# Diagonal blocks of the row maxima: the causal mask moves from a matmul to a GpSimd addition, with a copy on ScalarE between, and the maxima are taken for two heads at once

## The reference

```python
h = _layernorm(x, axis=-1) * (1 + ca) + sa
# attention, for each of 16 heads:
scores = jnp.einsum('bhqd,bhkd->bhqk', q, k) * scale
scores = jnp.where(causal, scores, jnp.finfo(scores.dtype).min)
attn = jax.nn.softmax(scores, axis=-1)
out = jnp.einsum('bhqk,bhkd->bhqd', attn, v)
...
x = x + ga * attention(h)
h = _layernorm(x, axis=-1) * (1 + cb) + sb
x = x + gb * soft_mixture_of_experts(h)
```

## Time and profile before

| | |
|---|---|
| Three runs | 3223.44, 3226.12, 3234.1 us; median 3226.12 |
| The profiled execution | 3226.97 us |
| Its span, first to last instruction | 3225.1 us |
| Granted TensorE clock, mean | 0.986 |
| Busy share: PE, PEld, DVE, ACT, POOL | 94%, 48%, 70%, 54%, 11% |

### The profile page before, as it was taken

One profiled execution on the slowest core, in us unless ns is written; L12 is line 12 of the kernel. 1 busy time (PEld: TensorE's weight loads), 2 busy tenths in 40 slices (PEclk: granted clock), 3 DMA queues, 4 the chain that ended last, 5 costly groups with the idle time before them and its releaser, 6 DMA issues.

```text
span 3225.1 us, 45179 instructions
## 1 busy us (share of the span) xinstructions
PE 3028.2 (94%) x17474; PEld 1535.5 (48%) x17651; DVE 2249.3 (70%) x4388; ACT 1754.8 (54%) x3189; POOL 340.8 (11%) x196
## 2 busy tenths in 40 slices
PE   6699999989999999998999999999999999999899
PEld 4233334447653333454774333345477333334468
DVE  5888887572778878756388888866448888885722
ACT  3356666564236666645515666664541666665550
POOL 4100000320400000112040000011222000002200
PEclk9899999999999999999999999999999999999999
DMA  5222201015412220002542202000453221100052
GB/s 153 79 41 41 41 1 40 15 57 205 150 35 34 41 41 27 21 7 92 196 138 54 41 1 41 28 21 7 145 178 116 41 41 26 17 27 27 33 180 75
DMA packets 124260, 206.12 MB, mean 64 GB/s; under 512 B 10223, under 2 KB 107189, under 8 KB 120425
## 3 DMA queue, kind: packets, MB, share of 16 engines
q1 hardware_dynamic: 110460, 153.07, 14.5%
q10 hardware_dynamic: 13584, 50.15, 8.4%
HBM read 160.21 MB, written 42.19 MB: 63 GB/s over the span
## 4 chain that ended last, share of the span: by engine, by line
PE 76%; DVE 15%; ACT 5%; issue 2%; ACTq 1%; DMA 1%; POOL 0%; SPq 0%; DVEq 0%
PE ps L737 14%; DVE pm L1347 12%; PE ps L717 9%; PE ps L642 9%; PE ps L904 7%; PE ps L843 7%; PE ps L655 7%; PE ps L935 4%; PE ps L602 3%; PE ps L924 3%; ACT R L1047 2%; PE ps L783 2%; PE ps L676 2%; PE ps L634 2%; PE ps L856 2%
## 5 line engine op out<-in xcount | busy, mean ns | idle before, releaser
L1347 DVE TENSOR_REDUCE pm<-ps 128x1 f32<-128x512 f32 (+4 forms) x2560 | 1380.5, 603 | 292.1 <-PE ps L642 193.5
L1047 ACT ACTIVATE R<-ps 128x512 f32<-128x512 f32 (+1 forms) x2240 | 1177.3, 592 | 652.0 <-PE ps L717 425.0
L717 PE MATMUL ps<-R 99*128 99x512 bf16 (+3 forms) x2560 | 829.8, 350 | 17.6 <-ACT R L1047 7.8
L642 PE MATMUL ps<-R 96*128 96x512 bf16 x1536 | 580.9, 386 | 39.4 <-DVE pm L1347 34.6
L737 PE MATMUL ps<-R 128*17 128x512 f32 (+3 forms) x5120 | 531.6, 533 | 4.9
L642 PEld LDWEIGHTS ps<-R 96*128 96x128 bf16 x1536 | 147.7, 97 | 437.3 <-DVE pm L1347 363.0
L717 PEld LDWEIGHTS ps<-R 99*128 99x128 bf16 x2560 | 241.9, 98 | 155.1 <-ACT R L1047 67.1
L655 PE MATMUL ps<-R 128*128 128x257 f32 x1024 | 247.2, 382 | 7.2 <-ACT R L991 3.6
L737 PEld LDWEIGHTS ps<-R 128*17 128x17 f32 x5120 | 118.2, 97 | 281.9 <-issue 168.4
L904 PE MATMUL ps<-R 128*128 128x512 f32 x512 | 230.0, 611 | 18.0 <-ACT R L1119 18.0
L843 PE MATMUL ps<-snT,R 128*128 128x512 f32 x512 | 230.1, 593 | 0.0
(11 more groups left out here) (159 smaller groups left out, 3142.8 us busy)
## 6 DMA issues: line engine op xcount, KB each, us to landing
R<-in_L_ffn_w_dram SPq DMA_DIRECT2D x64, 1024.0 KB, 6.1
R<-q_parts ACTq DMA_DIRECT2D x12, 768.0 KB
R<-k_parts ACTq DMA_DIRECT2D x12, 768.0 KB
q_parts<-R SPq DMA_DIRECT2D x16, 512.0 KB, 3.6
k_parts<-R SPq DMA_DIRECT2D x16, 512.0 KB, 3.5
R<-in_L_attn_x_dram SPq DMA_DIRECT2D x4, 2048.0 KB, 8.7
x_park<-R SPq DMA_DIRECT2D x16, 512.0 KB, 2.6
R<-x_park SPq DMA_DIRECT2D x16, 512.0 KB, 5.5
```

Source lines behind the costliest of these rows:

```text
L642: last = mm(ps[:, bank, :], qt(4 * c + r), kt(4 * kc, 4), start=True, stop=True)
L717: last = mm(bank[:, i * w:(i + 1) * w], kst[g % 2][0:BROWS, h0 + i, j * P:(j + 1) * P], qst[g % 2][0:BROWS, h0 + i, (c + 1) * CH - w:(c + ...
L1047: A(Eb[s % ESLOTS][:, h0:h0 + n, 0:w], ps[:, u % NST, 0:n * w].rearrange("p (n w) -> p n w", n=n), ACT.Exp, scale=SCALE).then_inc(s_ex, 1)
L1347: mx = lambda o, i: V.tensor_reduce(o, i, AX.X, ALU.max)
```

## The change

- PE writes a diag unit without the mask: four matmuls, each starting its part of the bank anew.
- ACT copies the bank to SBUF (`copied_diagonal`), in one of two buffers `mdiag`, each for a pair of heads. The bank is free for PE after this copy.
- POOL adds `maskb` in place (`masked_diagonal`).
- DVE reduces a pair at once, 128 x 1024 to eight maxima: heads 0 and 1 after the "even" unit of head 1, heads 2 and 3 after the chunk's last unit and before `negmax`.
- In `MAXES` the diag unit of head `h + 1` stands before the "odd" unit of head `h`.
- PE waits, three places back, for ACT's copy (`s_dgc`) or DVE's reduction (`s_mxf`), whichever kind of unit that was.
- `mdiag` lies on memory that a rotary set uses, so the first copy of a batch waits for the transfers that park that set.
- In the turn of a batch ACT's last rotary conversions (`parts(b + 1, 7)`) and its stores stand between the copies.

```diff
 def max_units_of_chunk(k):
     c = k % NC
+    yield k, 0, "diag", 0, 0
     for h in range(HG):
-        yield k, h, "diag", 0, 0
+        if h + 1 < HG:
+            yield k, h + 1, "diag", 0, 0
         yield k, h, "odd", 0, 0
...
-                pe.wait_ge(s_mxf, b * MU + (m + 1))
+                if m >= NMX:
+                    if m - NMX in DIAGONALS:
+                        pe.wait_ge(s_dgc, b * ND + diagonals_to(m - NMX))
+                    else:
+                        pe.wait_ge(s_mxf, b * DU + others_to(m - NMX))
...
                 elif kind == "diag":
-                    mm(ps[:, bank, :], identb[:, :], maskb[:, :, :].rearrange("p r t -> p (r t)"),
-                       start=True, stop=True)
                     for i in range(4):
-                        last = mm(ps[:, bank, i * P:(i + 1) * P], qt(4 * c + i), kt(4 * c + i, 1),
-                                  start=False, stop=True, skip_group_check=True)
+                        last = mm(ps[:, bank, i * P:(i + 1) * P], qt(4 * c + i), kt(4 * c + i, 1), start=True, stop=True)
...
+            def copied_diagonal(b, m):
+                if MAXES[m][2] != "diag":
+                    return
+                i = DIAGONALS.index(m)
+                if i == 0:
+                    act.wait_ge(s_pk[2], set_parked(b, max(j for j in range(QU) if set_of(b, j) == 2)))
+                if i >= 4:
+                    act.wait_ge(s_dgm, b * ND // 2 + i // 2 - 1)
+                act.wait_ge(s_mx, b * MU + m + 1)
+                nc.scalar.copy(mdiag[i // 2 % 2][:, i % 2, :, :].rearrange("p r t -> p (r t)"), ps[:, NST + m % NMX, :]).then_inc(s_dgc, 1)
...
                 for u, (s, h0, n, w) in enumerate(UNITS):
+                    while m < MAXES_BY[b][u]:
+                        copied_diagonal(b, m)
+                        m += 1
...
+            def masked_diagonal(b, m):
+                if MAXES[m][2] != "diag":
+                    return
+                i = DIAGONALS.index(m)
+                v = mdiag[i // 2 % 2][:, i % 2, :, :]
+                pool.wait_ge(s_dgc, b * ND + i + 1)
+                G.tensor_tensor(out=v, in0=v, in1=maskb[:, :, :], op=ALU.add).then_inc(s_dga, 1)
...
-                if kind == "diag":
-                    last = mx(of[:, :, 0], ps[:, bank, :].rearrange("p (r t) -> p r t", t=P))
...
                 last.then_inc(s_mxf, 1)
+                if (kind, h) == ("even", 1) or m in LAST_MAX:
+                    i = 2 * k + (m in LAST_MAX)
+                    dve.wait_ge(s_dga, b * ND + 2 * i + 2)
+                    mx(pm[:, k % 2, 2 * (i % 2):2 * (i % 2) + 2, :, 0], mdiag[i % 2]).then_inc(s_dgm, 1)
```

More of the change, by code:

```diff
@@ L91, with diagonals_to, others_to @@
 MU = len(MAXES)
+DIAGONALS = [m for m in range(MU) if MAXES[m][2] == "diag"]
+ND = len(DIAGONALS)
+DU = MU - ND
+def diagonals_to(m):
+    return sum(d <= m for d in DIAGONALS)
+def others_to(m):
+    return m + 1 - diagonals_to(m)
 ROWS_AT = [next(m for m, x in enumerate(MAXES) if x[0] == k and x[2] == "rows") for k in range(NK)]
@@ L267, in adaln_block @@
         vall = view(R2, 8192, NT * H * VC).rearrange("p (t h c) -> p t h c", t=NT, h=H)
+        mdiag = [view(R3, 1024 * i, 1024).rearrange("p (h r t) -> p h r t", h=2, r=4) for i in range(2)]
         outT = [view(R2, 12800 + 512 * i, 512) for i in range(2)]
@@ L368, in adaln_block @@
         s_mxf = sem("max_block_reduced")
+        s_dgc = sem("diagonal_block_copied")
+        s_dga = sem("diagonal_block_masked")
+        s_dgm = sem("two_heads_diagonals_reduced")
         s_nm = sem("negmax_parts_ready")
@@ L495, in load_bias @@
                     g, c = divmod(k, NC)
-                    sp.wait_ge(s_mxf, b * MU + (ROWS_AT[k] + 1 + NMX))
+                    sp.wait_ge(s_mxf, b * DU + others_to(ROWS_AT[k]))
                     for h in range(HG):
@@ L794, in beside @@
                     if x == 0:
-                        pe.wait_ge(s_mxf, (b + 1) * MU + NMX)
+                        pe.wait_ge(s_mxf, (b + 1) * DU)
                         pe.wait_ge(s_wog, b + 1)
@@ L1024, in _ @@
                     values(0, 2 * (i - 2) + 1)
+            for m in range(early_of(0)):
+                copied_diagonal(0, m)
             act.wait_ge(s_w3, 32)
@@ L1030, in _ @@
             for b in range(B):
-                if b:
-                    for i in range(8):
+                m = early_of(b)
+                for i in range(8):
+                    if b:
                         values(b, i)
+                    while m < values_by(b, i):
+                        copied_diagonal(b, m)
+                        m += 1
                 def evacuate(k):
@@ L1162, in _ @@
                         modulated(b + 1, c)
-                    for i in range(QU):
+                    for i in range(QU - 1):
                         parts(b + 1, i)
@@ L1166, in _ @@
                             store(0)
-                    for c in range(1, NC):
-                        store(c)
+                    for n in range(FIRST_WITH_MAXES, NT):
+                        for m in range(early_by(n - 1) if n > FIRST_WITH_MAXES else 0, early_by(n)):
+                            copied_diagonal(b + 1, m)
+                        if n == FIRST_WITH_MAXES:
+                            parts(b + 1, QU - 1)
+                        if n % 4 == 3:
+                            store(n // 4)
                 else:
@@ L1211, in _ @@
                 if b:
+                    for m in range(EARLY):
+                        masked_diagonal(b, m)
                     pool.wait_ge(s_cm, b * NT)
@@ L1214, in _ @@
                 if b == 0:
+                    for m in range(early_of(0)):
+                        masked_diagonal(0, m)
                     pool.wait_ge(s_psm, 1)
                     G.tensor_tensor(out=rnorm[:, 0:E], in0=ssq[:, 0:E], in1=neghalf[:, 0:E], op=ALU.pow).then_inc(s_psd, 1)
+                for m in range(early_of(b), MU):
+                    masked_diagonal(b, m)
                 def ln2_deviation(c):
@@ L1338, in reduce_unit @@
                 bank = NST + m % NMX
+                if kind == "diag":
+                    return
                 if kind == "rows":
@@ L1347, in reduce_unit @@
                 mx = lambda o, i: V.tensor_reduce(o, i, AX.X, ALU.max)
-                if kind == "diag":
-                    last = mx(of[:, :, 0], ps[:, bank, :].rearrange("p (r t) -> p r t", t=P))
-                elif kind == "odd":
+                if kind == "odd":
                     mx(of[:, 1, 1:2], ps[:, bank, 0:P])
@@ L1361, in negmax @@
             def negmax(b, k):
-                dve.wait_ge(s_mxf, b * MU + (LAST_MAX[k] + 1 + NMX))
+                dve.wait_ge(s_mxf, b * DU + others_to(LAST_MAX[k]))
+                dve.wait_ge(s_dgm, b * ND // 2 + 2 * (k + 1))
                 V.tensor_reduce(negm[:, :, :], pm[:, k % 2, :, :, 0:2 + k % NC], AX.X, ALU.max, negate=True).then_inc(s_own_nm, 1)
@@ L1397, in _ @@
             V.tensor_copy(maskTb[:, :, :], pmaskT.unsqueeze(1).to_broadcast([P, HG, P])).then_inc(s_id, 1)
-            V.sem_inc(s_mxf, NMX)
             for m in range(early_of(0)):
```

## The result

The changed kernel took 3358.2 us (median of four runs, 3354.1 to 3362.8) against 3227.6 us for the kernel before beside it: a ratio of 1.040, 95% interval 1.038 to 1.043. So 131 us were added, where 24 were predicted; the sign was right and the size was not.

What follows compares the result with a forecast made beforehand. PE was taken to pace about three quarters of the time, DVE most of the rest. Terms -41 - 4 + 8 + 6 + 5 + 14 + 36 = +24 us gave 3250 us, 0.7% slower, range 3204 to 3286.

Steps and rivals of the forecast that it cites:

- place 3: Chunk ends: POOL's masks hold `negmax`, rows unit 1.2 us late at 60 ends; bounds 0 and 72, half taken, +36 us.
- the pairs: DVE's reductions of two heads at once: +8 us for lumps, less 4 us for DVE's shorter work.
- PE loses the mask matmul: PE saves 0.22 us per diag unit, 55 us counted, taken at PE's 75% of the chain: -41 us.
- ACT's time: ACT's 256 bank copies, some 133 us of them in attention, delay scores: +6 us.
- place 1: Start of batch 0: copies wait for the transfer parking the last rotary set, delaying the first score: +5 us, once.
- place 2: Three batch turns: masks behind POOL's last rotary part delay DVE's tile 8 and PE: 4.7 us each, +14 us.
- by that alone 1118.0, no change: At a chunk end, the pair reduction ahead of `negmax` by itself leaves the rows unit's start unchanged: no cost.
- Faster: Rival: `negmax` is not held by POOL, so the 36 us term goes: 3214 us, or 3200; chance 0.24.
- Much slower: Rival: ACT becomes the bound, costing 33 us instead of 6, or DVE lumps cost 30: 3290 us and more; chance 0.08.

Runs made afterwards that it cites:

- 1: Kernel before with its 256 mask matmuls left out and nothing in their place: 3196.8 us, ratio 0.9915.
- 8: Kernel after without POOL's additions; DVE reduces each diag unit in its bank, ACT copies the mask from SBUF for nobody: 3208.5 us, ratio 0.9943.
- 7: Kernel after without POOL's additions, DVE reducing each head's copied diagonal apart instead of in pairs: 3221.0 us, ratio 0.9980.
- 3: Kernel after with POOL's 256 additions left out, DVE waiting for ACT's copies instead: 3253.0 us, ratio 1.0089.
- 4: Kernel after with one more wait: POOL's first mask of a chunk waits for the previous chunk's `negmax`: 3269.6 us, ratio 1.0140.
- 2: Kernel after with the old mask matmul put back on PE ahead of the four block matmuls, result unused: 3356.2 us, ratio 1.0415.
- 5: Kernel before with two unread POOL additions of 128x512 put on `negmax` at 52 chunk ends: 3372.4 us, ratio 1.0452.
- 12: Kernel before with one more unread DVE reduction of 1456 elements amid `negmax` at 52 chunk ends, nothing added on POOL: 3348.5 us, ratio 1.0390.
- 13: Kernel after with four useless PE matmuls of 512 columns before each of 64 waits for `negmax`: 3314.2 us, ratio 1.0274.

## Why the prediction was wrong

Two steps failed. The last of place 3 took half of the reckoned lateness of `negmax`, 36 us, and 85 were measured. And the pairs were priced at 4 us net by a share of the chain, and 35 were measured. Each row is the difference between two kernels, from their ratios, beside the terms that the prediction had for it.

| Part | Predicted, us | Measured, us | Between |
|---|---|---|---|
| PE loses the mask matmul | -41 | -27 | kernel before and 1 |
| ACT's time | +6 | +9 | 1 and 8 |
| Banks and reductions that wait for a copy | +5 (place 1) | +12 | 8 and 7 |
| Pairs | +8 - 4 | +35 | 7 and 3 |
| POOL outside `negmax` | +14 (place 2) | +16 | 3 and 4 |
| POOL on `negmax` | +36 (place 3) | +85 | 4 and kernel after |
| Sum | +24 | +130 | |

The sizes depend on the order in which the parts are taken: the mask matmul is worth 27 us in the kernel before, while giving it back to the kernel after changed nothing (2).

- **PE's term, -41: mis-sized, -27.** It counted PE's share of the chain (75%) as exposure; 27 of 56 us is one half. Where DVE sets the bank's release, a shorter unit mostly lengthens a wait: those for DVE grew by 47 us (1).
- **Pairs, +8, less 4 for DVE's shorter work: wrong, +35.** The bounds were 0 and 64, and I priced a pair by DVE's average share of the chain. But one pair in two stands straight ahead of `negmax`. The step that failed is in place 3: "by that alone 1118.0, no change". Without POOL, PE waited for `negmax` 46 times, 39.6 us (experiment 3), and with each head apart 3.3 us (7).
- **ACT, +6: about right for its time (+9)**; of the 12 us for banks and reductions that wait for a copy, 4.7 are place 1, and the other 7 had no term.
- **Place 1, +5: right in mechanism, 6.6 measured.** The copies began at 108.27 us where I had 106.3.
- **Place 2, +14: right, 15 measured, 16 by experiments.** In the first turn of the kernel after:

```profile
923.84 4.49 POOL L1258 TENSOR_TENSOR R<-R,maskb 128x512 f32<-128x512 f32 x4
...
926.14 1.22 DVE L1416 TENSOR_REDUCE pm<-R 128x8 f32<-128x1024 f32 x1 [4.54 <-POOL R L1258]
...
929.33 0.28 PE L664 MATMUL ps<-R 96*128 96x256 bf16 x1 [3.50 <-DVE pm L1416]
```

  DVE waits 4.54 us ahead of tile 8 (forecast 4 to 5), and PE's even unit of head 3 waits 3.50 us (forecast 3.8).
- **Place 3, +36: the mechanism was right, the size was not, +85.** Three things went into it. At the chunk end shown the masks came earlier than I placed them (1114.83 to 1117.10, not 1116.1 to 1118.7), and the first cast was held, which I had left out as not shown; the lengthening, 0.97 us at 54 ends, is less than the 1.2 at 60 that I reckoned. I halved it for time in which PE has other work, but 85 us were lost for 52.2 of lengthening. And it was priced at one us per us at the most, where experiments 5 and 12 measured 1.6 and 1.5. What the sum had at nothing was the clock: behind many of PE's waits came a stretch at 1.2 GHz, and keeping PE busy in them gave 42 us back (13).
- **The rivals.** "Faster" needed `negmax` not held in more than four ends of five; it was held in 54 of 64. "Much slower", 3290 us and more at a chance of 0.08, is where the time fell, but not by its main cause: it had named ACT, which cost 9 us of its own, and lumps on DVE of 30 us, near the 35 measured. The sign came out as forecast. All six rows of the table came out dearer than their terms, so the errors lay on one side and none hid another. The upper end of the range took 72 us as the most that place 3 could cost, and 85 lay beyond it.

The Trainium skill ("SBUF — State Buffer", Who interferes with whom) says that a DVE instruction with two SBUF inputs contends with a GpSimd instruction that reads SBUF, that a cast can contend too, and that a reduction does not on this chip. All three parts are borne out here: the subtraction up to 1.08 us, the cast up to 1.19 us, the pair reduction at 1.21 us beside a running addition.

What stays open: how the 7 us that remain between experiments 8 and 7 divide between banks and copies, and how much of the 85 us is clock and how much the wait. The stretches at 1.2 GHz are 225 us in the kernel after and 131 us in experiment 4, so by half the difference the clock took at most 47 of the 85 us, as an estimate; the other 38 or more are waits.

## What to carry to other kernels

An average share of the chain is a poor price. It gave 41 us for 256 matmuls that were worth 27, and 4 us for pairs that cost 35, since half of them land ahead of a small serial step on which the next stage waits. Such work is priced at that step, by what the next stage waits there. Before moving work to POOL, list DVE's small SBUF operations beside it, casts too, and keep the two apart with a wait on POOL: here one such wait was worth 85 us. And when PE sets the pace, count a stall of one or two us at about one and a half times its length (1.6 and 1.5 in experiments 5 and 12), and look at the stretches at the lower clock, not at waits alone.

## What the runs showed of the hardware

- A cast of 16 values a partition from float32 to bfloat16 in SBUF took 0.174 us alone and up to 1.193 us beside POOL's addition.
- A reduction of 128 x 1024 in SBUF took 1.21 us beside POOL's addition, as it does elsewhere.
- POOL's addition of a bfloat16 and a float32 operand of 128 x 512 took 1.16 us, its subtraction of two float32 operands 1.27 us. Whether the type or the operation makes the difference was not tried.
- Behind waits of PE of 1.0 to 2.4 us amid dense matmuls the granted clock fell to 1.2 GHz in 27 short stretches of attention, 116 us in all, against 3 and 10 us before; 37 other waits of over 1 us in attention had none. 56 us of useless matmuls ahead of the waits for `negmax` left 2 stretches, 10 us, and made the kernel 42 us faster.
